# A causal mask moved from TensorE to VectorE, and value projections moved behind the context products

## What is computed

```python
x = x + layernorm(attn_ref(layernorm(x), Wq, bq, Wk, bk, Wv, bv, Wo, bo))   # x: 2 x 1024 x 256, 16 heads of 128

q, k, v = heads(h @ Wq.T + bq), heads(h @ Wk.T + bk), heads(h @ Wv.T + bv)
q, k = apply_rope(q), apply_rope(k)
scores  = einsum('bhqd,bhkd->bhqk', q, k) / sqrt(128)
scores  = where(tril(ones(S, S)), scores, finfo.min)          # the causal mask
weights = softmax(scores)
context = einsum('bhqk,bhkd->bhqd', weights, v)
out     = merged(context) @ Wo.T + bo
```

## Time and profile before

| | |
|---|---|
| median of 3 runs | 1905.16 us (1902.91 to 1907.54) |
| profiled execution, its own time | 1904.82 us |
| its span, first to last instruction | 1903.1 us |
| mean granted TensorE clock over the span | 0.948 |
| PE busy | 1654.3 us (87%) |
| DVE busy | 1383.8 us (73%) |
| ACT busy | 1129.0 us (59%) |
| POOL busy | 667.5 us (35%) |
| the first attention's units | about 80 to 960 us of the span |

### The profile page before, as it was taken

One profiled execution on the slowest core, in us unless ns is written; L12 is line 12 of the kernel. 1 busy time (PEld: TensorE's weight loads), 2 busy tenths in 40 slices (PEclk: granted clock), 3 DMA queues, 4 the chain that ended last, 5 costly groups with the idle time before them and its releaser, 6 DMA issues. The chain is left out here.

```text
span 1903.1 us, 43770 instructions
## 1 busy us (share of the span) xinstructions
PE 1654.3 (87%) x14612; PEld 1020.7 (54%) x14612; DVE 1383.8 (73%) x2882; ACT 1129.0 (59%) x2158; POOL 667.5 (35%) x756
## 2 busy tenths in 40 slices
PE   3899999999999999999827745899999999982997
PEld 1577777777777777777713422233333333341554
DVE  4487777778777777777766564888888888837564
ACT  4566666666666666666545641266666666666444
POOL 0654554555455555545221123021212222223011
PEclk9899999999999999999968967899999999995998
DMA  4322111112111111211000010000000000001000
GB/s 130 88 54 49 41 47 43 43 41 52 47 41 47 44 41 41 52 47 34 17 0 1 1 36 9 17 13 15 15 13 16 12 18 11 8 1 66 1 23 22
DMA packets 53107, 61.83 MB, mean 32 GB/s; under 512 B 11345, under 2 KB 32018, under 8 KB 53010
## 3 DMA queue, kind: packets, MB, share of 16 engines
q1 hardware_dynamic: 53010, 60.55, 13.1%
HBM read 18.57 MB, written 2.10 MB: 11 GB/s over the span
## 5 line engine op out<-in xcount | busy, mean ns | idle before, releaser
L1566 ACT ACTIVATE a_prob<-psum 128x1024 f32<-128x1024 f32 (+3 forms) x384 | 302.3, 813 | 212.1 <-PE psum L1523 209.5
L1606 DVE TENSOR_REDUCE a_mx<-psum 128x1 f32<-128x512 f32 (+3 forms) x608 | 367.5, 655 | 61.2 <-PE psum L1505 55.0
L1598 POOL TENSOR_SCALAR_AFFINE_SELECT a_prob<-a_prob 128x256 f32<-128x256 f32 x256 | 103.8, 406 | 420.5 <-ACT a_prob L1566 418.0
L1502 PE MATMUL psum<-a_kd,a_qp 128*128 128x512 f16 (+3 forms) x768 | 217.5, 337 | 34.2 <-DMA a_kd<-a_k_part 22.6
L528 POOL TENSOR_TENSOR a_swp<-a_swp,a_sin 128x512 f32<-128x512 f32 x128 | 163.1, 1274 | 161.6 <-DMA a_swp<-a_lin 161.6
L884 DVE TENSOR_REDUCE a_nmax<-psum 128x1 f32<-128x1024 f32 (+7 forms) x256 | 191.3, 748 | 1.0 <-PE psum L599 1.0
L532 POOL TENSOR_TENSOR a_rope<-a_swp,a_cosd 128x512 f32<-128x512 f32 x128 | 164.2, 1283 | 12.4 <-POOL a_swp L528 4.7
L224 POOL TENSOR_TENSOR x<-x,y (+1 forms) x64 | 54.4, 879 | 319.5 <-ACT y L196 319.5
L1544 PE MATMUL psum<-a_prob,a_vg 128*32 128x512 f32 (+3 forms) x1536 | 165.4, 503 | 0.8 <-ACT a_o_sb L1572 0.4
L1502 PEld LDWEIGHTS psum<-a_kd,a_qp 128*128 128x128 f16 x768 | 70.7, 98 | 173.3 <-DVE a_mx L1606 94.4
L756 ACT ACTIVATE a_prob_big<-psum,a_nmax 128x1024 f32<-128x1024 f32 (+3 forms) x128 | 121.8, 952 | 68.5 <-DVE a_nmax L884 65.1
(11 more groups left out here) (256 smaller groups left out, 4477.8 us busy)
## 6 DMA issues: line engine op xcount, KB each, us to landing
a_swp<-a_lin SPq DMA_DIRECT2D x256, 128.0 KB, 2.3
a_qp<-a_q_part SPq DMA_DIRECT2D x192, 16.0 KB
a_kd<-a_k_part SPq DMA_DIRECT2D x192, 16.0 KB
x<-_attn_hidden_states_dram SPq DMA_DIRECT2D x4, 512.0 KB, 5.5
a_w_raw<-in_L_attn_Wq_dram SPq DMA_DIRECT2D x16, 128.0 KB, 2.3
a_w_raw<-in_L_attn_Wk_dram SPq DMA_DIRECT2D x16, 128.0 KB, 2.3
a_w_raw<-in_L_attn_Wv_dram SPq DMA_DIRECT2D x16, 128.0 KB, 2.3
a_wo_raw<-in_L_attn_Wo_dram SPq DMA_DIRECT2D x1, 2048.0 KB
```

The costliest lines, as they stand in the source:

```text
L1502: last = pe.matmul(to[:, j * n:(j + 1) * n], qp[:, w % 3, t * P:(t + 1) * P], kd[:, w % 3, j0 + j, a:e], start=True, stop=not edge)
L1566: act.activation(prob_at(u, i)[:, 2 * pair:2 * pair + 2, a % BANK:a % BANK + e - a], c.psum[:, pair_of(u, i):pair_of(u, i) + 2, 0:e - a], ...
L1606: dve.tensor_reduce(mx[:, t, j0:j0 + per, a // BANK], work(("S", w, i))[:, 0:per * (e - a)].rearrange("p (j n) -> p j n", j=per), AX.X, AL ...
```

## The change

The mask's product on PE goes. Ahead of each maximum DVE adds `mask_qk` in place, in PSUM, onto the 128 diagonal columns, and waits on a new semaphore for its own result before it reduces the row. The two `vals` on PE, which stood ahead of `context` in slots 2 and 3, stand behind it; their waits move with them.

```diff
@@ score (PE)
                         for m, (qq, kk) in enumerate(((hi[0], hi[1]), (hi[0], lo[1]), (lo[0], hi[1]))):
-                            last = pe.matmul(scores(p, a, e), qq[:, b, rows], kk[:, b, a:e], start=(m == 0), stop=(m == 2 and e < n))
-                    last = pe.matmul(scores(p, n - P, n), c.ident_b[:, :], c.mask_qk[:, :], start=False, stop=True)
+                            last = pe.matmul(scores(p, a, e), qq[:, b, rows], kk[:, b, a:e], start=(m == 0), stop=(m == 2))
                     last.then_inc(scored, 1)
@@ unit (PE)
                             out(u - 1, h - 1 + b, 2)
-                        if p == 2 and exists(u + 1):
-                            if exists(u - 1):
-                                pe.wait_ge(y_done, 4 * (u - 1) + 3)
-                            else:
-                                pe.wait_ge(cos_ready, 5)
-                            vals(u + 1, h + b, 1 - b, 0)
-                        if p == 3 and exists(u + 1):
-                            if exists(u - 1):
-                                pe.wait_ge(y_done, 4 * (u - 1) + 4)
-                            else:
-                                pe.wait_ge(cos_ready, 8)
-                            vals(u + 1, h + b, 1 - b, 1)
                         if p == 4 and exists(u + 2):
...
                             out(u - 1, h - 1 + b, 3)
+                        if p == 2 and exists(u + 1):
+                            if exists(u - 1):
+                                pe.wait_ge(y_done, 4 * (u - 1) + 3)
+                            else:
+                                pe.wait_ge(cos_ready, 5)
+                            vals(u + 1, h + b, 1 - b, 0)
+                        if p == 3 and exists(u + 1):
+                            if exists(u - 1):
+                                pe.wait_ge(y_done, 4 * (u - 1) + 4)
+                            else:
+                                pe.wait_ge(cos_ready, 8)
+                            vals(u + 1, h + b, 1 - b, 1)
@@ maximum (DVE)
                     dve.wait_ge(scored, 8 * u + p + 1)
+                    edge = scores(p, BLOCKS[p] * P - P, BLOCKS[p] * P)
+                    dve.tensor_tensor(edge, edge, c.mask_qk[:, :], ALU.add).then_inc(edge_masked, 1)
+                    dve.wait_ge(edge_masked, 8 * u + p + 1)
                     dve.tensor_reduce(nmax[:, b, p:p + 1], scores_row(p), AX.X, ALU.max, negate=True).then_inc(max_done, 1)
```

More of the change, by code:

```diff
@@ L433, in attention_0 @@
         vals_made, vhi_ready, v_ready = sem("vals_made"), sem("vhi_ready"), sem("v_ready")
-        scored, max_done, exp_done = sem("scored"), sem("max_done"), sem("exp_done")
+        scored, edge_masked, max_done, exp_done = sem("scored"), sem("edge_masked"), sem("max_done"), sem("exp_done")
         turned, pt_hi_done, pt_lo_done = sem("turned"), sem("pt_hi_done"), sem("pt_lo_done")
```

## The result

The changed kernel takes 1946.21 us (median of 4 runs, 1945.47 to 1946.55) against 1904.05 us for the kernel before (4 runs, 1902.91 to 1907.54). The ratio is 1.0218, with a 95% interval of 1.020 to 1.0235: slower by 42 us. The forecast was 1951 us, the range 1919 to 1976.

What follows compares the result with a forecast made beforehand. The prediction took a DVE-ACT ring (26.5 us a unit) and PE's work (26.9) as near-equal bounds. Masks add 82 us, PE's hold-ups give 35 back, less some 1 us at the start: +46, 1951 us, range 1919 to 1976.

Steps and rivals of the forecast that it cites:

- ring of DVE and ACT: First attention's units: `turned_lo`, maximum, exponent and `turned_hi` wait for each other, once a slot; 26.5 us a unit unmasked.
- the first view: Busy times in the first attention's units: PE busy 821 of 844 us, which looks like a stage bound by PE.
- rival A: PE is the bound and the masks hide in DVE's idle time: -38 us, 1866 us; chance 5%.
- Part 1: Mask's product off PE: 0.056 us each, 0.45 us a unit, 14.3 us if PE is the bound.
- Part 2: `vals` behind `context`: the 0.81 us stall in slot 2 fits beneath the context products, 24 us if PE is the bound.
- Part 3: Mask on DVE inside the ring in each slot: delays the maximum by 0.32 us, bounds 0.20 and 0.41 us.
- rival C: DVE's wait for its own mask result is free, 0.20 us a mask: +16 us, 1921 us; chance 9%.
- The sum: Ring 29.1 us a unit against PE's 26.4; 82 us of masks less 35 us back, +46 us with the edges.
- 1.17 off: Average time a unit that PE holds up the ring in slots 3, 6 and 7; returned over 30 units, 35 us.
- B: Rival: half of the slots have overlooked slack, so cost and gain cancel, within 4 us of 1905; chance 4%.
- D: Rival: PE's clock falls as PE waits more; at a mean clock of 0.85, 2010 us; chance 4%.
- PE's waits: PE arrives about 2.7 us a unit early and waits in several pieces of about half a us, replacing the stall.

Runs made afterwards that it cites:

- e1: The kernel before with only the two `vals` moved behind `context`, the mask still a product on PE: 1879.9 us, ratio 0.9871.
- e6: The changed kernel with the mask on DVE for odd `p` alone, a product on PE for the others: 1903.2 us, ratio to the kernel before 0.9998.
- e4: The changed kernel with the mask's product put back on PE as well, so the mask is added twice: 1946.3 us.
- e2: The kernel before with only the mask moved to DVE, the two `vals` still ahead of `context`: 1951.2 us, ratio 1.0238.
- e5: The changed kernel with the mask's addition made twice on DVE, each waiting for the one before: 2027.7 us.
- e3: The changed kernel with the mask's addition ahead of `turned_lo(p+1)` in DVE's queue: 1906.9 us.

## Why the prediction was right, by its own steps

**What bounds the kernel.** Right. The prediction held that a ring of DVE and ACT and the work of PE lay within 2% of each other, 26.5 and 26.9 us a unit. e1 shows the one at 26.92 (26.77 of it products), the slots of e1, e6 and the changed kernel the other at 26.4. Had the first view been all, PE busy for 97%, the forecast would have been rival A's.

**Part 1, the product.** Right: worth 0.056 us each to PE (842.84 - 830.05 = 12.8 us of busy time in e4) and nothing to the kernel (e4).

**Part 2, the values' products.** Right that the stall would fit beneath the context if PE were the bound (24 us forecast, 25 in e1), and that it brings nothing itself under the masks. The sentence that it would give `context_hi` back in time was right in the changed kernel; e2 shows that this is worth 5 us there, since PE would have been early enough in every other unit in either order.

**Part 3, the mask.** The size was right: 0.32 us forecast, 0.29 us long with the maximum 0.32 to 0.33 us behind it. In the table of slots the first mask costs 0.33 in six of the eight; slot 6, where PE's hold-up lies over it, fits the same (2.90 - 0.23 + 0.33 = 3.00, measured 2.99). What was wrong is slot 0, with 0.11. The mask's write into PSUM takes about as long as the write of the same shape into SBUF (288 to 299 ns against 281 to 292 for `turned_lo(1)`). The rule of the Trainium skill that the prediction weighed against this (page "VectorE: DVE Perf Modes", section "The DRAIN you can't avoid"), a wait of DVE for itself that is free, doesn't hold for this addition: the next operation starts 0.32 to 0.34 us after it with the wait (e5), and 0.21 us after it without one (e3). That is rival C, and e5's 2027.7 us instead of 2000 excludes it.

**The sum.** The forecast was a unit of 29.1 us; it is 28.88. The unit grew by 1.20 us, which is 8 x 0.33 less 1.44; the forecast took 1.17 off. That term was right for what it named: PE gave back 0.61 and 0.93 us in slot 3, 0.23 in slot 6 and 0.17 in slot 7. Two pieces were missing. The larger is slot 0, where the prediction charged a full mask because `weight_lo` on DVE closes the slot. It read this the wrong way round: the end of `weight_lo` hangs on POOL, so the slot had 0.22 us of slack, in each unit. The smaller is slot 2 (3.05 us now, from 523.43 to 526.48), a fourth place where PE had held up the ring, ahead of `turned_hi(4)`; it gave back 0.13 us in every second unit. Against that the additions cost 0.01 us each more than thought. Net -0.2 x 31 = -6 us, which with the edges gives +42 for +46.

**The rivals.** A, at 1866 us, needed a mask under 0.15 us on the ring. B needed slack in half of the slots; only slot 0 had any, 0.22 us. D did not occur, the clock stayed at 1.00. PE's waits come in several pieces, as expected, 2.5 us a unit in all where 2.7 were forecast. But I had put them ahead of the transposes and of `vals` alone: the transposes have 1.0 us of them, the values' products 0.57, and the longest single one, 0.78 us in each unit, is ahead of the first context product (at 544.14), which by the code waits until `context_lo` has emptied bank 5 (its row ends at 544.04).

## What to carry to other kernels

An engine that is 97% busy can hide a second bound right behind it: look for two engines whose waits release each other in turn, add up their steps over a period, and compare that sum with the busy engine's work before moving anything onto either. Work moved off a full engine onto one with a fifth of its time idle cost 46 us here, because it was put between the steps of such a ring; the same instruction in a place where its engine waits anyway was free, as long as its input was there in time (the narrow rows; for the wide ones it was not). Check, too, what the last operation of each step itself waits for: where its end hangs on a third engine, as that of `weight_lo` does on POOL, work put ahead of it can cost next to nothing. And test the halves of a change apart: here one half alone made the kernel 1.3% faster.

## What had not been expected of the hardware

A two-input DVE operation on SBUF (128x256, `weight_lo`) takes 0.41 us when POOL is idle and 0.68 to 1.32 us when it starts beside POOL's 128x512 product: it then ends 0.28 to 0.29 us after that product's row, whenever it started. POOL's product itself keeps to 1.26 to 1.29 us either way. The mask, with one input and its output in PSUM, kept to 0.29 to 0.30 us throughout (the 256 of the changed kernel lie between 288 and 299 ns).
